# Attention step of a post-norm transformer layer: a new fixed order of the same instructions on all five queues

## The chip, the cores and the metric

The kernel runs on one core of a Trainium2 chip. The metric is the time of one execution on the device in microseconds (us), as the median of several runs. The engines of a core are TensorE (PE; its weight loads are listed apart as PEld), VectorE (DVE), ScalarE (ACT), GpSimd (POOL) and SyncE (SP, which only issues transfers). Each works through its own queue in order and waits on semaphores for the others.

## The reference, cut to what matters

```python
# x: (4, 1024, 256), 16 heads of 64
proj = x @ W_in.T + b_in                       # q, k, v
q, k = _rope(q, sin, cos), _rope(k, sin, cos)
att = einsum('bhqd,bhkd->bhqk', q, k) * scale  # causal mask, softmax
y = einsum('bhqk,bhkd->bhqd', att, v)
x = _layernorm(x + y @ W_out.T + b_out)
...
x = _layernorm(x + ffn(x))                     # 16 experts, top 3 of them by token
```

## The kernel before, in words

The program has four parts, one behind the other: attention, routing, experts, and the last sum with its norm. The change touches the first alone.

Attention is done for one pair of heads of one batch at a time: 4 batches by 8 pairs make 32 steps. A step is a set of named events, and its events are spread over several *turns* of a software pipeline. In each turn every engine runs through a fixed list of events, one list per queue. A mark behind an event tells of which step it is: none for the step of this turn, one + for the next step, ++ for the one after, - for the one before. So the lists alone decide in which order a queue works; what an event waits for is written in its own code and is the same wherever it stands. The turns are numbered from -2 to 32, and -2, -1, 0, 30, 31 and 32 are not full.

The events, by queue (q is 0 to 11, and .0 or .1 is the head of the pair):

- PE: **F** projections (F0, F1 for q and k, 12 matmuls of 512 columns; F2, F3 for v, 12 of 256). **A q.h** first-pass unit: scores for the maximum of each row (`a_ps`, L600). **X0, X1** transposes of the negated maxima (`t_ps`, L709). **B q.h** second-pass unit: the scores again, with the keys on the partitions, as two matmuls (`b_ps`, L607 and L608); its width goes 512, 384, 256, 128, 512 x5, 384, 256, 128 for q = 0 to 11. **V q** value product of both heads (`y_ps`, L689); V0 to V3 make one half of the output, V4 to V11 the other. **D** denominators (`t_ps`, L699). **O** output product, normalised values by W_out (`t_ps`, L714).
- ACT: **E q.h** the exponential of a second-pass unit (L799), **w** maxima out of `t_ps`, **h** the high half of roped q and k, **v**, **N**, **d** other evictions, **y** the norm of finished rows.
- DVE: **M q.h** maximum of a first-pass unit (L918, L922), **C** joins maxima, **r** the two products of the rotary embedding, **k** partial sums of probabilities (L956 to L961), **R** reciprocals, **G** multiplication by them (L971), **o** adds an output product to the rows (L981), **z** statistics of the norm.
- POOL: **a** and **l**, sum and low half of the embedding, **T** the causal cut of a diagonal block (L521), **K** partial sums (L535), **u** roots for the norm, **p** a bias.
- SP: **W** and **S** put the halves to memory and load them stacked, **L** loads weights and x.

The events V and D are matmuls with 64 output columns (`128*64` in the profile): the two heads lie side by side in TensorE's array. All others use 128 columns or, in X, 8. `a_ps`, `b_ps` have one bank per head, so that a unit waits until the unit before it of the same head has been read: A by M, B by E. `t_ps` is one bank for X, D and O, and each of these waits for the reader of the one before (`wait_misc`). The statistics z are there in the second and third turn behind the end of each of the first three batches, u in the fourth, y in the fifth and sixth, p in the third to the sixth.

Of the kernel before, what the change touches and what calls it, by code (L numbers as in the profile page):

```python
# [31 lines left out]
def parse(text):  # L32

    return [(w.rstrip("+-"), w.count("+") - w.count("-")) for w in text.split()]


PE_ORDER = parse("""B0.0 A0.0+ B0.1 A0.1+ A1.0+ B1.0 A1.1+ A2.0+ B1.1 X1 B2.0 A2.1+ A3.0+ B2.1 F0++ B3.0 A3.1+ D1- V8- V9- V10-
V11- B3.1 B4.0 A4+ B4.1 F1++ A5.0+ B5.0 V0 V1 V2 D0 V3 B5.1 B6.0 A5.1+ O1- A6.0+ B6.1 B7.0 X0+ A6.1+ B7.1
A7.0+ B8.0 V4 V5 V6 V7 B8.1 A7.1+ B9.0 O2- B9.1 B10.0 A8.0+ F2++ A8.1+ B10.1 A9.0+ O3- B11 A9.1+ A10.0+ O0
A10.1+ A11.0+ F3++ A11.1+""")  # L40
ACT_ORDER = parse("""E0.0 E0.1 E1.0 E1.1 E2.0 w1 E2.1 E3.0 d1- h0++ N1- E3.1 E4.0 E4.1 y0 h1++ E5.0 d0 h2++ E5.1 E6.0 N0 E6.1 y1 E7.0
w0+ E8.0 E7.1 h3++ E8.1 y2 E9.0 E9.1 y3 E10.0 v2++ E10.1 E11.0 E11.1 v3++""")
DVE_ORDER = parse("""M11.1 M0.0+ C0 M0.1+ M1.0+ M1.1+ M2.0+ k0 M2.1+ M3.0+ k1 k2 r0++ M3.1+ R4- r1++ R5- M4.1+ k3 M4.0+ R6- R7-
M5.0+ r2++ G1- r3++ z0 M5.1+ o1- M6.0+ R0 M6.1+ R1 M7.0+ R2 R3 G0 z1 M7.1+ o2- M8.0+ M8.1+ M9.0+ o3- M9.1+ M10.0+
o0 M10.1+ M11.0+""")
POOL_ORDER = parse("""K11- u0 T0 u1 T1 u2 T2 u3 a0++ l0++ T3 a1++ l1++ p0 a2++ l2++ K5 a3++ K6 l3++ K7 T8 T9 K8 T10 K9 T11 K10""")
SP_ORDER = parse("""L1+ S3+ L0++ W0++ S0++ W1++ S1++ S2++""")

UNITS = 12
ON_DIAGONAL = (0, 1, 2, 3, 8, 9, 10, 11)  # L50
# [3 lines left out]
LN_STATS, LN_ROOTS, LN_APPLY, LN_STORE = 1, 3, 4, 6  # L54
MISC = [(e, ahead) for e, ahead in PE_ORDER if e[0] in "XOD"]


def both(event):
    return [event + ".0", event + ".1"] if event[0] in "AB" else [event]


PE_ORDER = [(e, ahead) for event, ahead in PE_ORDER for e in ([event] if "." in event else both(event))]

# [30 lines left out]
def index_of(event):  # L94
    return int(event[1:].split(".")[0])
# [39 lines left out]
def attention_phase(nc, A, dram, shared):  # L135
# [4 lines left out]
    with ExitStack() as ctx:  # L140
# [120 lines left out]
        def turns(turn, order, last=None):  # L261
            for it in range(-2, STEPS + 1):
                turn(it, it % 4, last if last and it == STEPS else order)
# [8 lines left out]
        def _(sp):  # L272
# [117 lines left out]
            def turn(it, place):  # L390

                for i, (e, ahead) in enumerate(SP_ORDER):
                    n, s, c = it + ahead, (place + ahead) % 2, index_of(e)
# [54 lines left out]
        def _(pool):  # L448
# [87 lines left out]

            turns(turn, POOL_ORDER)

        @block.tensor
        def _(pe):  # L540
# [205 lines left out]

            turns(turn, PE_ORDER, PE_LAST)

        @block.scalar
        def _(act):  # L750
# [102 lines left out]

            turns(turn, ACT_ORDER, ACT_LAST)

        @block.vector
        def _(dve):
# [127 lines left out]
            dve.wait_ge(m["bias_in"], 16 * 9)  # L985
            turns(turn, DVE_ORDER)

# [861 lines left out]
```

## Time and profile before

| | |
|---|---|
| median of 3 runs | 1830.77 us (1829.52 to 1833.35) |
| the profiled execution | 1833.15 us, span 1831.4 us |
| busy in the span | PE 1685.0, DVE 1385.9, POOL 1232.3, ACT 729.2 us |
| attention, 60 to 1275 us | PE busy 1187.38 of 1215.00 us, DVE 1023.61, POOL 898.95, ACT 554.86; granted clock 0.99 |
| routing, 1275 to 1420 us | PE busy 104.12 of 145.00 us |
| experts and last sum, from 1420 us | PE busy 361.24 of 412.00 us |

In the timeline, a matmul's bar is longer than the time for which it holds the array, since matmuls overlap. What the next one has to wait is read from start to start. A row with "xN" holds N matmuls that follow each other.

### The profile page before, as it was taken

Reading aid. Unit: us, or ns where it says so; the run is one execution under the profiler, and the core shown is the slowest. Engines: PE = TensorE matmul, PEld = TensorE weight load, DVE = VectorE, ACT = ScalarE, POOL = GpSimd, SP = SyncE. Lnnn points to the kernel's source line nnn. Section 1 sums busy time; section 2 is a strip of 40 time slices with the busy share of each in tenths; the row PEclk is TensorE's granted clock in tenths of the full one; section 3 lists DMA queues with packets and bytes.
Section 4 is the critical chain, followed back from the end, with each engine's and each line's share of the span. In section 5 each row is a group of like instructions: output and inputs, shape, how many; then the busy total and the mean of one; then the engine's idle time right before and its main releaser. Section 6 shows DMA issues by size and latency. Waiting matters only on the chain. (4 is left out here: it accounts for less than half of the span.)

```text
span 1831.4 us, 34003 instructions
## 1 busy us (share of the span) xinstructions
PE 1685.0 (92%) x9489; PEld 1263.0 (69%) x9490; DVE 1385.9 (76%) x3230; ACT 729.2 (40%) x1549; POOL 1232.3 (67%) x1062
## 2 busy tenths in 40 slices
PE   4699999999999999999999999998659999999990
PEld 4566667666766677666766676664339999999980
DVE  3578888888888888988888888875775665665554
ACT  2234444444445544445444444543352222222222
POOL 3256788677877787788767787765016777777764
PEclk8799999999999999999999999999759999999995
DMA  9976566655665777556776565541964444444448
GB/s 303 343 204 164 156 167 200 182 168 154 186 161 165 232 220 199 147 170 192 204 236 187 161 186 149 153 113 49 337 191 69 74 71 73 74 72 71 73 63 277
DMA packets 185379, 302.10 MB, mean 165 GB/s; under 512 B 23600, under 2 KB 82736, under 8 KB 185120
## 3 DMA queue, kind: packets, MB, share of 16 engines
q1 hardware_dynamic: 161872, 269.20, 49.6%
q0 software_dynamic: 21312, 30.02, 10.3%
q10 hardware_dynamic: 2064, 1.31, 0.3%
q8 instruction: 60, 0.98, 0.2%
q14 instruction: 71, 0.58, 0.1%
HBM read 188.67 MB, written 111.54 MB: 164 GB/s over the span
## 5 line engine op out<-in xcount | busy, mean ns | idle before, releaser
L799 ACT ACTIVATE prob<-b_ps 128x512 f32<-128x512 f32 (+3 forms) x768 | 354.6, 488 | 354.7 <-PE b_ps L608 262.2
L535 POOL TENSOR_TENSOR acc<-acc,prob 128x1024 f32<-128x1024 f32 (+1 forms) x192 | 354.6, 1847 | 6.4 <-POOL acc L535 5.7
L607 PE MATMUL b_ps<-q,k 128*128 128x512 f32 (+3 forms) x768 | 294.9, 388 | 5.6 <-ACT prob L799 3.0
L508 POOL TENSOR_TENSOR roped<-rot 128x512 f32<-128x512 f32 x128 | 175.0, 1367 | 165.8 <-DVE rot L938 165.0
L600 PE MATMUL a_ps<-k,q 128*128 128x512 f32 (+3 forms) x768 | 266.0, 383 | 17.1 <-DMA k<-scratch_hilo 6.4
L918 DVE CUSTOM_DVE_ANT_0 masked<-a_ps,causal 128x256 bf16<-128x256 f32 (+3 forms) x512 | 245.9, 496 | 45.2 <-PE a_ps L600 37.8
L689 PE MATMUL y_ps<-prob,v_sb 128*64 128x512 f32 (+3 forms) x1536 | 274.2, 492 | 0.1
L608 PE MATMUL b_ps<-q,k 65*128 65x512 f32 (+3 forms) x768 | 264.7, 348 | 0.0
L1495 POOL DMA_INDIRECT scratch_sum<-y,dst_i x111 | 185.5, 1671 | 95.6 <-ACT y L1567 89.4
L967 DVE RECIPROCAL inv<-inv 128x128 f32<-128x128 f32 x256 | 232.2, 929 | 7.7 <-ACT inv L840 5.3
L513 POOL TENSOR_TENSOR lo<-roped,hi 128x512 fp32r<-128x512 f32 x128 | 176.1, 1376 | 80.3 <-ACT hi L812 80.3
L689 PEld LDWEIGHTS y_ps<-prob,v_sb 128*64 128x64 f32 x1536 | 104.6, 137 | 180.4 <-issue 175.6
L1521 PEld LDWEIGHTS h_ps<-mxT,w_now 128*128 128x128 f32 x1776 | 218.3, 194 | 5.6
L1521 PE MATMUL h_ps<-mxT,w_now 128*128 128x128 f32 x1776 | 218.7, 277 | 0.0
L1530 PE MATMUL yo_ps<-w,hT 128*128 x888 | 209.9, 379 | 0.0
L592 PE MATMUL g_ps<-xT,w_sb 128*128 128x512 f32 x768 | 194.1, 403 | 8.1 <-DVE rot L938 5.1
L607 PEld LDWEIGHTS b_ps<-q,k 128*128 128x128 f32 x768 | 145.2, 189 | 73.9 <-issue 42.8
L922 DVE TENSOR_REDUCE max_b<-a_ps 128x1 f32<-128x512 f32 (+1 forms) x256 | 163.1, 638 | 35.3 <-PE a_ps L600 32.8
L600 PEld LDWEIGHTS a_ps<-k,q 128*128 128x128 f32 x768 | 143.0, 192 | 59.7 <-DVE max_b L922 11.6
L1480 POOL DMA_INDIRECT xin<-scratch_xn,src_i x111 | 110.7, 997 | 106.0 <-POOLq L1009 72.5
L592 PEld LDWEIGHTS g_ps<-xT,w_sb 128*128 128x128 f32 x768 | 147.8, 196 | 40.3 <-DVE rot L938 6.2
L1530 PEld LDWEIGHTS yo_ps<-w,hT 128*128 128x128 f32 x888 | 160.1, 190 | 17.2
(258 smaller groups left out, 2396.3 us busy)
## 6 DMA issues: line engine op xcount, KB each, us to landing
q<-scratch_hilo SPq DMA_DIRECT2D x192, 256.0 KB, 4.5
k<-scratch_hilo SPq DMA_DIRECT2D x192, 256.0 KB, 5.2
scratch_hilo<-hi SPq DMA_DIRECT2D x64, 512.0 KB, 3.9
scratch_hilo<-lo SPq DMA_DIRECT2D x64, 512.0 KB, 4.6
w_sb<-scratch_wsplit SPq DMA_DIRECT2D x32, 512.0 KB, 3.6
w<-in_L_ffn_W_dram SPq DMA_DIRECT2D x32, 512.0 KB, 9.8
wv_sb<-scratch_wsplit SPq DMA_DIRECT2D x16, 512.0 KB, 6.0
xT<-scratch_xsplit SPq DMA_DIRECT2D x6, 1024.0 KB, 6.8
```

What stands on the lines that cost most here:

```text
L535: nc.gpsimd.tensor_tensor(sums, old, probs(q), ALU.add).then_inc(m["sum_p"], 1)
L592: ins = nc.tensor.matmul(out, left, right, start=(a, b, k) == PRODUCTS[0], stop=(a, b, k) == PRODUCTS[-1], skip_group_check=True)
L600: nc.tensor.matmul(out, q1[s][:, h, blk * P:(blk + 1) * P], k1[s][:, h, k0:k0 + w], start=True, stop=True, skip_group_check=True).then_inc ...
L607: nc.tensor.matmul(out, k1[s][:, h, js], q1[s][:, h, qs], start=True, stop=False, skip_group_check=True)
L608: ins = nc.tensor.matmul(out, k2[s][0:65, h, js], q2[s][0:65, half, h, 512 - w:512], start=False, stop=True, skip_group_check=True)
L689: ins = nc.tensor.matmul(y_ps[64 * h:64 * h + 64, 512 - w:512], v_sb[:, pairs, j, s, 64 * h:64 * h + 64], probs(q)[:, h, :], start=(j == 0 ...
L799: nc.scalar.activation(probs(q)[:, h, :], b_ps[:, h, 0:w], ACT.Exp).then_inc(exp_done[h], 1)
L918: nc.vector.tensor_tensor_reduce(masked[:, h, 0:w], a_ps[:, h, 0:w], causal[:, 512 - w:512], -1.0, -MASKED, ALU.add, ALU.min, out).then_in ...
L967: nc.vector.reciprocal(part, part).then_inc(inv_done[c], 1)
L1495: pool.indirect_dma_start(out=dram[f"sum{t % SUMS}"], out_offset=bass.IndirectOffsetOnAxis(ap=dst_i[:, t:t + 1], axis=0), in_=y[:, t % 2, ...
L1521: ins = nc.tensor.matmul(h_ps[:, s, c * P:(c + 1) * P], w1_now[:, s, k, c * P:(c + 1) * P], xT[:, s, k * P:(k + 1) * P], start=(k == 0), s ...
L1530: ins = nc.tensor.matmul(yo_ps[:, s, 0:D], hT[:, s, c * P:(c + 1) * P], w2[:, bass.ds(e, 1), c, :].rearrange("p a d -> p (a d)"), start=(c ...
```

## The change

The lists of the five queues are replaced. Nothing else is: the same events, the same waits, tiles and buffers.

```diff
-PE_ORDER = parse("""B0.0 A0.0+ B0.1 A0.1+ A1.0+ B1.0 A1.1+ A2.0+ B1.1 X1 B2.0 A2.1+ A3.0+ B2.1 F0++ B3.0 A3.1+ D1- V8- V9- V10-
+PE_ORDER = parse("""B0.0 A0.0+ B0.1 A0.1+ A1.0+ X1 B1.0 A1.1+ A2.0+ B1.1 A2.1+ B2.0 A3.0+ B2.1 F0++ B3.0 D1- A3.1+ V8- V9- V10- V11-
...
-DVE_ORDER = parse("""M11.1 M0.0+ C0 M0.1+ M1.0+ M1.1+ M2.0+ k0 M2.1+ M3.0+ k1 k2 r0++ M3.1+ R4- r1++ R5- M4.1+ k3 M4.0+ R6- R7-
+DVE_ORDER = parse("""M11.1 M0.0+ C0 M0.1+ M1.0+ M1.1+ M2.0+ k0 M2.1+ M3.0+ k1 r0++ M3.1+ R4- r1++ R5- M4.0+ M4.1+ R6- k2 R7- k3 r2++
...
-POOL_ORDER = parse("""K11- u0 T0 u1 T1 u2 T2 u3 a0++ l0++ T3 a1++ l1++ p0 a2++ l2++ K5 a3++ K6 l3++ K7 T8 T9 K8 T10 K9 T11 K10""")
-SP_ORDER = parse("""L1+ S3+ L0++ W0++ S0++ W1++ S1++ S2++""")
+POOL_ORDER = parse("""K11- u0 T0 u1 T1 u2 a0++ u3 l0++ T2 T3 a1++ p0 l1++ a2++ l2++ K5 a3++ K6 l3++ K7 T8 K8 T9 T10 K9 T11 K10""")
+SP_ORDER = parse("""L1+ L0++ S3+ W0++ S0++ S1++ W1++ S2++""")
```

PE in the first third of a full turn, before: B3.0, A3.1+, D1-, V8- to V11- (each V and D two matmuls, one for each head).

```order
L607 MATMUL b_ps<-q_0,k_0 128x128
L608 MATMUL b_ps<-q_0,k_0 128x128
L600 MATMUL a_ps<-k_1,q_1 128x512
L699 MATMUL t_ps<-acc,ones 64x512 x2
L689 MATMUL y_ps<-prob,v_sb 64x512 x2
L689 MATMUL y_ps<-prob,v_sb 64x384 x2
```

The same place of the changed kernel:

```order
L607 MATMUL b_ps<-q_0,k_0 128x128
L608 MATMUL b_ps<-q_0,k_0 128x128
L699 MATMUL t_ps<-acc,ones 64x512 x2
L600 MATMUL a_ps<-k_1,q_1 128x512
L689 MATMUL y_ps<-prob,v_sb 64x512 x2
L689 MATMUL y_ps<-prob,v_sb 64x384 x2
```

The first-pass unit A3.1+ has moved in between the denominators D1- and the value products. They stood as one stretch of 64-column matmuls, and are two now.

PE in the middle of the turn, before: B7.0, X0+, A6.1+, B7.1, A7.0+, B8.0, V4 to V7.

```order
L608 MATMUL b_ps<-q_1,k_1 128x512
L709 MATMUL t_ps<-ident,max_a 8x128
L600 MATMUL a_ps<-k_0,q_0 128x512
L607 MATMUL b_ps<-q_1,k_1 128x512
L608 MATMUL b_ps<-q_1,k_1 128x512
L600 MATMUL a_ps<-k_0,q_0 128x256
L607 MATMUL b_ps<-q_1,k_1 128x512
L608 MATMUL b_ps<-q_1,k_1 128x512
L689 MATMUL y_ps<-prob,v_sb 64x512 x8
L607 MATMUL b_ps<-q_1,k_1 128x512
```

The same place of the changed kernel: B7.0, A6.1+, V4, X0+, B8.0, A7.0+, B7.1, V5 to V7.

```order
L608 MATMUL b_ps<-q_1,k_1 128x512
L600 MATMUL a_ps<-k_0,q_0 128x512
L689 MATMUL y_ps<-prob,v_sb 64x512 x2
L709 MATMUL t_ps<-ident,max_a 8x128
L607 MATMUL b_ps<-q_1,k_1 128x512
L608 MATMUL b_ps<-q_1,k_1 128x512
L600 MATMUL a_ps<-k_0,q_0 128x256
L607 MATMUL b_ps<-q_1,k_1 128x512
L608 MATMUL b_ps<-q_1,k_1 128x512
L689 MATMUL y_ps<-prob,v_sb 64x512 x6
L607 MATMUL b_ps<-q_1,k_1 128x512
```

V4 stands alone, ahead of the transpose X0+, and B8.0 comes ahead of B7.1.

DVE in the first third of the turn, before: k1, k2, the two products of r0++, and M3.1+.

```order
L958 TENSOR_TENSOR acc<-prob 128x2x384
L961 TENSOR_TENSOR acc<-acc,prob 128x2x256
L938 SCALAR_TENSOR_TENSOR rot<-g_ps,bias,cos_sb 128x512
L938 SCALAR_TENSOR_TENSOR rot<-g_ps,bias,sin_sb 128x512
L918 ISA masked,max_a<-a_ps,causal 128x512
```

DVE of the changed kernel, some rows later: R5-, M4.0+ and M4.1+, R6-, k2, R7-, k3.

```order
L967 RECIPROCAL inv<-inv 128x128
L922 TENSOR_REDUCE max_b<-a_ps 128x1 x2
L967 RECIPROCAL inv<-inv 128x128
L961 TENSOR_TENSOR acc<-acc,prob 128x2x256
L967 RECIPROCAL inv<-inv 128x128
L961 TENSOR_TENSOR acc<-acc,prob 128x2x128
```

The partial sum k2 (`128x2x256`) has moved from ahead of r0++ to a place behind R6-, and k3, which stood behind M4.1+, follows it behind R7-. On POOL, T2, for which k2 waits, has moved behind l0++ in the same way (lists above).

## Rows read from the trace of the kernel before

**Rows 1.** Windows of one undisturbed and one long turn: busy us (x instructions), clock.

```profile
282.60:319.20 36.60, 36.60 (x195) 25.55 (x194) 31.84 (x67) 17.14 (x37) 28.66 (x25) 1.00 0.66 188
503.00:541.00 38.00, 36.98 (x196) 25.51 (x195) 31.69 (x69) 16.79 (x37) 32.74 (x41) 1.00 0.53 150
```

**Rows 2.** One line's instructions: X1, 95 to 1240 us (duration, first and last start).

```profile
L709 PE MATMUL t_ps<-ident,max_c x31: 272/273/275, 102.5 to 1211.2; 128*8 128x128 f32 x31
```

**Rows 3.** Timeline of PE in the undisturbed turn: start us, us, instruction.

```profile
299.88 1.03 PE L699 MATMUL t_ps<-acc,ones 128*64 128x512 f32 x4
300.74 0.39 PE L689 MATMUL y_ps<-prob,v_sb 128*64 128x128 f32 x4
...
304.02 0.39 PE L608 MATMUL b_ps<-q,k 65*128 65x512 f32 x1
304.25 0.27 PE L709 MATMUL t_ps<-ident,max_a 128*8 128x128 f32 x1
...
305.21 0.28 PE L600 MATMUL a_ps<-k,q 128*128 128x256 f32 x1
305.33 0.40 PE L607 MATMUL b_ps<-q,k 128*128 128x512 f32 x1
305.57 0.39 PE L608 MATMUL b_ps<-q,k 65*128 65x512 f32 x1
305.89 3.65 PE L689 MATMUL y_ps<-prob,v_sb 128*64 128x512 f32 x16
...
309.82 0.39 PE L608 MATMUL b_ps<-q,k 65*128 65x512 f32 x1
```

**Rows 4.** Timeline of all engines, same turn: the weight load of B7.1.

```profile
304.64 0.19 PEld L607 LDWEIGHTS b_ps<-q,k 128*128 128x128 f32 x1 [0.19 <-ACT prob L799]
```

**Rows 5.** Timeline, a turn with statistics z: B7.0 and X0+.

```profile
487.42 0.39 PE L608 MATMUL b_ps<-q,k 65*128 65x512 f32 x1
...
488.31 0.27 PE L709 MATMUL t_ps<-ident,max_a 128*8 128x128 f32 x1 [0.49 <-DVE x1b L981]
```

**Rows 6.** Timeline, the turn with roots u: B4.1.

```profile
515.67 0.47 PE L607 MATMUL b_ps<-q,k 128*128 128x512 f32 x1 [1.02 <-ACT prob L799]
```

**Rows 7.** Timeline, a turn with the norm y: A7.0+ and B8.0.

```profile
563.73 0.28 PE L600 MATMUL a_ps<-k,q 128*128 128x256 f32 x1
...
564.13 0.19 PEld L607 LDWEIGHTS b_ps<-q,k 128*128 128x128 f32 x1 [0.44 <-ACT prob L799]
```

**Rows 8.** Waits of 95 to 1208 us: us in total, times, longest us.

```profile
PEld b_ps L607 <- ACT prob L799: 8.9, 36, 0.5
...
PEld a_ps L600 <- DVE max_a L918: 8.1, 41, 0.4
PEld t_ps L709 <- DVE x1b L981: 8.1, 16, 0.9
...
PE b_ps L607 <- ACT prob L799: 2.1, 4, 1.0
```

**Rows 9.** Timeline, the first microseconds of the turn: M1.0+ ends, A2.0+ loads.

```profile
284.55 0.09 DVE L918 DVE_READ_ACCUMULATOR2_ANT max_a<- 128x1 f32 x1
284.69 0.19 PEld L600 LDWEIGHTS a_ps<-k,q 128*128 128x128 f32 x1 [0.16 <-DVE max_a L918]
```

**Rows 10.** Timelines of DVE (G1-, G0) and POOL (K6) in the undisturbed turn.

```profile
299.81 0.67 DVE L971 TENSOR_TENSOR yT<-yT,inv 128x512 f32<-128x512 f32 x1
308.92 1.25 DVE L971 TENSOR_TENSOR yT<-yT,inv 128x512 f32<-128x512 f32 x1
...
307.26 2.36 POOL L535 TENSOR_TENSOR acc<-acc,prob 128x1024 f32<-128x1024 f32 x1
309.59 1.72 POOL L513 TENSOR_TENSOR lo<-roped,hi 128x512 fp32r<-128x512 f32 x1
```

**Rows 11.** Timeline of POOL in turn 31: T9, then K8.

```profile
1265.88 0.41 POOL L521 TENSOR_SCALAR_AFFINE_SELECT prob<-prob 128x256 f32<-128x256 f32 x1 [1.05 <-ACT prob L799]
1266.25 2.35 POOL L535 TENSOR_TENSOR acc<-acc,prob 128x1024 f32<-128x1024 f32 x1
```

More of the change, by code:

```diff
@@ L34, in parse @@
     return [(w.rstrip("+-"), w.count("+") - w.count("-")) for w in text.split()]
-PE_ORDER = parse("""B0.0 A0.0+ B0.1 A0.1+ A1.0+ B1.0 A1.1+ A2.0+ B1.1 X1 B2.0 A2.1+ A3.0+ B2.1 F0++ B3.0 A3.1+ D1- V8- V9- V10-
[L38 to L42, printed above, removed]
-DVE_ORDER = parse("""M11.1 M0.0+ C0 M0.1+ M1.0+ M1.1+ M2.0+ k0 M2.1+ M3.0+ k1 k2 r0++ M3.1+ R4- r1++ R5- M4.1+ k3 M4.0+ R6- R7-
-M5.0+ r2++ G1- r3++ z0 M5.1+ o1- M6.0+ R0 M6.1+ R1 M7.0+ R2 R3 G0 z1 M7.1+ o2- M8.0+ M8.1+ M9.0+ o3- M9.1+ M10.0+
-o0 M10.1+ M11.0+""")
-POOL_ORDER = parse("""K11- u0 T0 u1 T1 u2 T2 u3 a0++ l0++ T3 a1++ l1++ p0 a2++ l2++ K5 a3++ K6 l3++ K7 T8 T9 K8 T10 K9 T11 K10""")
-SP_ORDER = parse("""L1+ S3+ L0++ W0++ S0++ W1++ S1++ S2++""")
+PE_ORDER = parse("""B0.0 A0.0+ B0.1 A0.1+ A1.0+ X1 B1.0 A1.1+ A2.0+ B1.1 A2.1+ B2.0 A3.0+ B2.1 F0++ B3.0 D1- A3.1+ V8- V9- V10- V11-
+A4+ B3.1 B4.0 F1++ A5.0+ B4.1 B5.0 A5.1+ V0 V1 D0 V2 V3 B5.1 B6.0 O1- A6.0+ B6.1 B7.0 A6.1+ V4 X0+ B8.0 A7.0+
+B7.1 V5 V6 V7 B8.1 A7.1+ O2- A8.0+ B9.0 A8.1+ B9.1 F2++ B10.0 B10.1 A9.0+ O3- B11 A9.1+ A10.0+ O0 A10.1+ A11.0+
+F3++ A11.1+""")
+ACT_ORDER = parse("""E0.0 E0.1 E1.0 E1.1 E2.0 w1 E2.1 E3.0 d1- h0++ N1- E3.1 E4.0 h1++ y0 E5.0 E4.1 d0 h2++ E5.1 E6.0 N0 E7.0 E6.1
+w0+ y1 E7.1 E8.0 h3++ y2 E8.1 E9.0 E9.1 y3 E10.0 E10.1 E11.0 E11.1 v2++ v3++""")
+DVE_ORDER = parse("""M11.1 M0.0+ C0 M0.1+ M1.0+ M1.1+ M2.0+ k0 M2.1+ M3.0+ k1 r0++ M3.1+ R4- r1++ R5- M4.0+ M4.1+ R6- k2 R7- k3 r2++
+G1- M5.0+ z0 r3++ M5.1+ o1- z1 M6.0+ R0 M6.1+ M7.0+ R1 R2 R3 G0 M7.1+ o2- M8.0+ M8.1+ M9.0+ o3- M9.1+ M10.0+ o0
+M10.1+ M11.0+""")
+POOL_ORDER = parse("""K11- u0 T0 u1 T1 u2 a0++ u3 l0++ T2 T3 a1++ p0 l1++ a2++ l2++ K5 a3++ K6 l3++ K7 T8 K8 T9 T10 K9 T11 K10""")
+SP_ORDER = parse("""L1+ L0++ S3+ W0++ S0++ S1++ W1++ S2++""")
 UNITS = 12
```

## The prediction

> **What bounds the kernel now.** I read the engines' busy shares first, then windows of one turn each, then TensorE's timeline in them, and last the list of waits. An undisturbed turn takes 36.60 us; TensorE is busy through all of it at the full clock of 2.4 GHz, DVE for 31.84, POOL for 28.66, ACT for 17.14 [rows 1]. So a turn ends when TensorE has worked through its list, and another engine counts where TensorE waits for it. Turns are not all that long: from the first X1 to the last, 30 turns later, 1108.7 us pass, 36.96 a turn [rows 2], and the longest fills its window of 38.00 without TensorE being busy throughout [rows 1]. The order can therefore act in two ways. It can change what a list costs TensorE when nothing is late, which repeats in every turn, and it can take away or bring waits, of which the bars hide many, so that they must be read from start to start.
>
> **The change, part one: boundaries.** Value products and denominators use 64 columns of the array, everything around them 128. Between the second halves of B8.0 and B8.1 lie 4.25 us (305.57 to 309.82) [rows 3]. Two second-pass matmuls at 0.24 each (305.33 to 305.57) and eight pairs of 64-column matmuls at 0.43 (299.88 to 300.74 is two pairs) come to 3.92. The stretch costs 0.33 us more than its work, for going in and coming out once. Before, a full turn has three such stretches: D1- with V8- to V11-, V0 to V3 with D0, V4 to V7. Now it has five, because A3.1+ stands between D1- and V8-, and X0+, B8.0, A7.0+ and B7.1 between V4 and V5. Moving D0 by one place inside its stretch, and O1-, O2- beside first-pass units, opens none.
>
> The first new boundary is there in the 30 turns that have both D1- and A3.1+. A3.1+ also loses a predecessor of 128 columns, which covers a weight load thinly, so I take 0.30 of the 0.33: 9.0 us. The second is there in 32 turns. There the array is left for a transpose with 8 columns of weights, where a load of 128 takes 0.19 [rows 4]; between 0.14 (all of that saved) and 0.33 I take 0.27, nearer the full price, since only the way out changes: 8.6 us. Together +17.6, and nothing hides it, for TensorE is the engine that never rests.
>
> The Trainium skill (TensorEngine Tiling (Array Packing), Key Properties) says that a change of tiling mode drains the engine, and gives no price. TensorE: Matmul & The Clock Gate puts the drain at some 128 cycles and a weight load at P / 1.2 ns; an estimate from it is 0.05 + 0.05 us going in and 0.05 + 0.11 coming out, 0.27 with rounding, so 62 boundaries would cost 16.7 at most. The sum above goes by the row.
>
> **Part two: waits that go.** B7.1 waits in undisturbed turns for its exponential E6.1, which stands on ACT behind the eviction N0 [rows 4]. In turns with the norm y, B8.0 waits for E7.0, which stands behind y1: 0.40 from A7.0+ to B8.0 against 0.12 [rows 7, 3], and the load in the open adds 0.1. Now V4, X0+, B8.0 and A7.0+ stand ahead of B7.1, and V4 (0.86 us) ahead of B8.0, and E7.0 ahead of E6.1 and y1. The waits of this pair come to 8.9 us in 36 [rows 8]. About three quarters of such a wait is lost time (0.38 of 0.44 in rows 7, less in the short ones), and some stand at the turn's start and stay: I take -6.
>
> X0+ must wait for o1-, which stands on DVE behind z0 in turns with statistics: 0.89 from B7.0 to it, against 0.23 [rows 5, 3], so 0.66 lost of a longest wait of 0.9. Its 16 waits are 8.1 us [rows 8]; 0.26 off each leaves 3.9. Behind V4 it comes 1.1 us later. All of it goes: -4. (On DVE, o1- itself comes later by z1 only behind it.)
>
> B4.1 waits for E3.1 in the turn with roots, since u0 to u3 hold up T2, k2, r0++, a0++ and h0++ one after the other: 1.02 us once, 2.1 in four waits [rows 6, 8], and some 0.1 each for the open load. Now r0++ stands ahead of k2, a0++ ahead of u3, and B4.1 stands behind F1. But l0++, T2 and so k3 come later, which D0 waits for, and a2++ and h2++, ahead of E5.1. Of 2.5 us I take back 1.5.
>
> At the end, turn 31 has no projections and waits on POOL's chain of sums. There K8 stands behind T9, which is 1.05 us late for its exponential [rows 11]; now K8 goes first: -1.0. Together -12.5.
>
> **Part three: waits that may come.** DVE used to do k2 while F0 ran; now its 0.7 us fall where DVE is full. Each of r2++, a2++ and h2++ comes a few tenths later, but so does TensorE, held up by the first boundary. E5.1 before B6.1, and k3 before D0, keep a few tenths of room. The tightest is A8.1+, which used to stand behind F2 and now stands ahead of it, 1.4 us earlier. It waits for M7.1+, which stands behind G0 on DVE. G0 takes 1.25 us and ends just after K6 on POOL does (309.62), while G1- takes 0.67 [rows 10]: a DVE sum of two SBUF operands stands still while POOL works. R1 to R3 now stand behind M7.0+, so G0 comes about 1 us later and may meet l3++ (1.3 us). Counting the queue through, A8.1+ would wait some 0.15 us in each of 29 full turns if it does, 0.3 at most, and nothing if it doesn't: 0 to 8.7, of which I take 2. X1 now stands two units earlier; it waits for C0, which ends in time in an undisturbed turn, and what it costs there is taken off the wait of A2.0+ behind it.
>
> The transfers move with the SP list (S3+ behind L0++, S1++ ahead of W1++), but are used a turn or more later: nothing, unless S3+ behind L0++'s wait for F1 came late, and it has half a turn.
>
> **The sum.** 17.6 - 12.5 + 2 = +7.1 us. On the profiled execution's 1833.15 that is 1840.3; it lies 2.4 above the median of the runs shown, so for the median I say 1830.8 + 7.1 = 1838.
>
> **The rivals.** *Slower still* (0.2): G0 meets l3++ in every turn and D0 or B6.1 wait too. For it: DVE is busy 31.84 of 36.60, and k2 lost its cover. Against: the longer turn gives the other engines 0.5 us more. 0.3 to 0.4 in 29 turns in place of the 2: 1845 to 1847.
>
> *No difference* (0.24): the boundary in front of or behind a single stretch costs less than that of the row, 0.2 say, since only two or four matmuls have to be covered, and all waits named go: 62 x 0.2 = 12.4, less 14 = -1.6, or some 1829 to 1834. The drain and loads that the Trainium skill's figures give lie between this and the row.
>
> *Faster* (0.11): the waits at the start of the turn go too. A2.0+ loads 0.05 us after M1.0+ ends at 284.64, having waited 0.16 [rows 9]; the waits for first maxima are 8.1 us in 41 [rows 8], and more lies hidden under the bars. X1, now in front, fills this time with work that had to be done anyway, and B2.0 follows sooner. If nothing else held F0 up, 0.3 us would come back in 29 turns: 1838 - 8.7 = 1829, and with the cheap boundary of the case before 1824. It decides at the start of F0: only if that comes more than 0.1 us sooner after B0.0 is it real. Against it: M1.0+, M1.1+ and M2.0+ follow each other on DVE without a gap, A3.0+ waits for M2.0+ as before, and their order has not changed.
>
> *As forecast* (0.45): 1834.5 to 1842.
>
> **Range and chances.** What a measurement of this kernel can tell from no change is about 0.2%, 3.7 us. Slower by more than that holds the forecast and the first rival, 0.65; within it 0.24; faster 0.11. Between 1829 and 1847 lies all but the faster rival and the far end of the slower one.
>
> **What would show it.** In the profile after: an undisturbed turn of 37.0 to 37.2 us; the second half of B3.0 to V8- longer by 0.3 besides the work that moved; V4 alone taking about 1.1 to 1.2 us until X0+; no wait of PEld of `t_ps` L709 for o1-, no 0.19 before B7.1; a wait of A8.1+ for `max_b` of 0 to 0.3; K8 in turn 31 right behind T8. I am wrong if a lone stretch costs under 0.2, if F0 starts sooner, or if a wait of over 0.3 us stands in every turn at a place that I have not named.

## The result: 0.7% slower, 1844.8 us against 1831.2

The changed kernel takes 1844.8 us in the median of 4 runs (1842.12 to 1845.83), the kernel before 1831.19 in the 4 runs beside them: a ratio of 1.0071, 95% interval 1.0054 to 1.0089, which is 10 to 16 us. The profiled execution of the changed kernel took 1843.8 us (span 1842.1), 10.7 above that of before. The forecast was +7, 1838, with a range to 1847.

On the page of the changed kernel PE is busy for 1691.9 us, DVE for 1380.7, ACT for 737.8 and POOL for 1229.4, much as before. Such sums tell nothing here; single turns do. Windows of an undisturbed turn, of a long one and of turns 1 to 29 together (columns as in [rows 1]; the third row has its match below it, from the kernel before):

```profile
400.48:437.48 37.00, 37.00 (x195) 25.52 (x194) 31.50 (x67) 17.40 (x37) 27.11 (x24) 1.00 0.59 172
288.24:325.94 37.70, 37.25 (x195) 25.33 (x194) 32.26 (x67) 17.25 (x37) 28.74 (x25) 1.00 0.62 182
138.56:1222.31 1083.75, 1077.25 (x5627) 737.29 (x5626) 930.46 (x1991) 514.16 (x1069) 826.54 (x736) 1.00 0.62 178
```

```profile
135.78:1208.48 1072.70, 1067.03 (x5627) 739.85 (x5626) 934.35 (x1991) 506.47 (x1069) 829.88 (x738) 1.00 0.63 180
```

Turns 1 to 29 are 11.05 us longer; the clock was full in both. Turn 1 also starts 2.8 us later (138.56 for 135.78), and behind turn 29 the changed kernel takes 3.1 us less, which together makes the 10.7 between the profiled executions. An undisturbed turn went from 36.60 [rows 1] to 37.00, inside the forecast 37.0 to 37.2, which makes 29 x 0.40 = 11.6. What turns take beyond that was 1072.70 - 29 x 36.60 = 11.3 us before, and is 1083.75 - 29 x 37.00 = 10.75 now. Here the forecast failed: it let most of the waits in disturbed turns go, and something as large has come instead.

**The boundaries.** PE's timeline in the undisturbed turn after, to be laid beside [rows 3]: D1- is alone between B3.0 and A3.1+, V4 between A6.1+ and X0+.

```profile
407.09 0.28 PE L608 MATMUL b_ps<-q,k 65*128 65x128 f32 x1
407.30 1.08 PE L699 MATMUL t_ps<-acc,ones 128*64 128x512 f32 x4
408.31 0.50 PE L600 MATMUL a_ps<-k,q 128*128 128x512 f32 x1
408.74 2.37 PE L689 MATMUL y_ps<-prob,v_sb 128*64 128x512 f32 x16
...
422.45 0.40 PE L600 MATMUL a_ps<-k,q 128*128 128x512 f32 x1
422.78 1.08 PE L689 MATMUL y_ps<-prob,v_sb 128*64 128x512 f32 x4
423.79 0.27 PE L709 MATMUL t_ps<-ident,max_a 128*8 128x128 f32 x1
```

The same place of the kernel before:

```profile
289.21 0.28 PE L608 MATMUL b_ps<-q,k 65*128 65x128 f32 x1
289.33 0.45 PE L600 MATMUL a_ps<-k,q 128*128 128x512 f32 x1
289.71 1.08 PE L699 MATMUL t_ps<-acc,ones 128*64 128x512 f32 x4
290.62 2.32 PE L689 MATMUL y_ps<-prob,v_sb 128*64 128x512 f32 x16
```

From the second half of B3.0 to V8- it was 290.62 - 289.21 = 1.41 us and is 408.74 - 407.09 = 1.65, 0.24 more, and the stretch that starts with V8- is 0.05 longer (2.37 for 2.32): 0.29 for D1-. V4 fills 1.01 us until X0+ (422.78 to 423.79), where its two pairs of matmuls take 0.86 inside a stretch [rows 3]: 0.15 more. A6.1+ to V4 takes 0.33, and a matmul of 512 columns 0.24 where no boundary follows: 0.09 on the way in. That makes 0.24 for V4 in this place, where the forecast took 0.27.

A start that comes sooner, which the "faster" rival wanted, is not there: F0 begins 3.80 us behind B0.0 (400.49 to 404.29), and it was 282.61 to 286.41 before. In the long turn it is 4.32 (288.25 to 292.57).

**The waits.** Waits in turns 1 to 29 of the kernel after (us in total, times, longest), beside [rows 8]. The waits of t_ps L709 for o1- (8.1 us in 16) are gone, as are PE's own 2.1 for the exponential. The 24 waits of PEld for an exponential are none of the old ones: they are B6.1's, 0.3 us, and B7.0's behind it, 0.19, in 12 turns. New are also that of X1 for `max_c`, in 12 turns, and A8.1+'s for `max_b`, in 2.

```profile
PEld b_ps L607 <- ACT prob L799: 6.0, 24, 0.3
PE t_ps L709 <- DVE max_c L929: 4.8, 12, 0.5
PEld a_ps L600 <- DVE max_b L918: 1.2, 2, 0.6
PE g_ps L592 <- DMA xT<-scratch_xsplit: 1.0, 2, 0.7
```

X1's wait stands in the long turns. The timeline of all engines in one of them shows K10 on POOL, the join C0 (L929) and M0.1+ behind it on DVE, then X1:

```profile
288.78 1.29 POOL L535 TENSOR_TENSOR acc<-acc,prob 128x512 f32<-128x512 f32 x1
...
289.27 0.82 DVE L929 TENSOR_TENSOR max_c<-max_b 128x8 f32<-128x8 f32 x1
...
290.02 0.28 DVE L918 CUSTOM_DVE_ANT_0 masked<-a_ps,causal 128x128 bf16<-128x128 f32 x1
...
290.25 0.27 PE L709 MATMUL t_ps<-ident,max_c 128*8 128x128 f32 x1 [0.45 <-DVE max_c L929]
```

C0 joins two lists of 8 values per partition, and takes 0.82 us: it ends at 290.09, with K10 (290.07). Its durations over the whole of attention (shortest, median, longest in ns, then first and last start):

```profile
L929 DVE TENSOR_TENSOR max_c<-max_b x31: 160/286/852, 99.7 to 1223.3; 128x8 f32<-128x8 f32 x31
```

### The profile page after: what moved, and what is told of

It reads as the page before. It is cut to its first block and busy times, and to the rows that moved or that the text cites. A ratio compares the mean times of both kernels' runs of the same rounds, so it can differ in the third digit from the quotient of the medians.

```text
span 1842.1 us, 34003 instructions
## 1 busy us (share of the span) xinstructions
PE 1691.9 (92%) x9489; PEld 1258.0 (68%) x9490; DVE 1380.7 (75%) x3230; ACT 737.8 (40%) x1549; POOL 1229.4 (67%) x1062
## 3 DMA queue, kind: packets, MB, share of 16 engines
q0 software_dynamic: 21312, 30.02, 10.2%
## 5 line engine op out<-in xcount | busy, mean ns | idle before, releaser
L535 POOL TENSOR_TENSOR acc<-acc,prob 128x1024 f32<-128x1024 f32 (+1 forms) x192 | 359.5, 1872 | 14.8 <-ACT prob L799 7.8
L600 PE MATMUL a_ps<-k,q 128*128 128x512 f32 (+3 forms) x768 | 276.5, 393 | 21.0 <-DMA k<-scratch_hilo 12.2
L607 PE MATMUL b_ps<-q,k 128*128 128x512 f32 (+3 forms) x768 | 284.0, 376 | 2.0 <-DMA q<-mrow 1.4
L689 PE MATMUL y_ps<-prob,v_sb 128*64 128x512 f32 (+3 forms) x1536 | 281.3, 494 | 0.0
L689 PEld LDWEIGHTS y_ps<-prob,v_sb 128*64 128x64 f32 x1536 | 99.0, 136 | 151.9 <-issue 125.8
L922 DVE TENSOR_REDUCE max_b<-a_ps 128x1 f32<-128x512 f32 (+1 forms) x256 | 157.1, 634 | 2.8 <-PE a_ps L600 2.8
```

What stands on the lines that cost most here:

```text
L535: nc.gpsimd.tensor_tensor(sums, old, probs(q), ALU.add).then_inc(m["sum_p"], 1)
L600: nc.tensor.matmul(out, q1[s][:, h, blk * P:(blk + 1) * P], k1[s][:, h, k0:k0 + w], start=True, stop=True, skip_group_check=True).then_inc ...
L607: nc.tensor.matmul(out, k1[s][:, h, js], q1[s][:, h, qs], start=True, stop=False, skip_group_check=True)
L689: ins = nc.tensor.matmul(y_ps[64 * h:64 * h + 64, 512 - w:512], v_sb[:, pairs, j, s, 64 * h:64 * h + 64], probs(q)[:, h, :], start=(j == 0 ...
```

## The experiments

All are timed beside the kernel before. Besides the ratio, the table has three times from the trace: from the first X1 to the last, 30 turns later (before: 1108.7 [rows 2]); turns 14 and 22, in which F1 needs the next batch's x; and the other 27 of turns 1 to 29, from each B0.0 to the next. The 27 turns repeat best: the changed kernel has 1007.2 and 1007.5 in its two traces, and 1007.9 and 1007.1 with another SP list. A difference there of more than a microsecond is taken for the edit's.

| kernel | median us | ratio (95%) | 30 turns | 27 turns | turns 14 and 22 |
|---|---|---|---|---|---|
| before | 1831.2 | 1 | 1108.7 | 999.0 | 73.7 |
| changed | 1844.8 | 1.0071 (1.0054 to 1.0089) | 1123.8 | 1007.2 | 76.6 |
| changed, once more | 1846.0 | 1.0073 (1.0057 to 1.0089) | 1123.5 | 1007.5 | 76.8 |
| changed, X1 back | 1846.4 | 1.0072 (1.0057 to 1.0086) | 1123.8 | 1005.5 | 78.9 |
| changed, C0 with one operand | 1842.0 | 1.0051 (1.0038 to 1.0064) | 1124.6 | 1002.3 | 82.4 |
| changed, old SP list | 1840.5 | 1.0046 (1.0032 to 1.0060) | 1120.3 | 1007.9 | 75.1 |
| changed, W1++ first on SP | 1838.8 | 1.0031 (1.0021 to 1.0042) | 1121.4 | 1007.1 | 75.1 |
| changed, both boundaries closed | 1842.3 | 1.0054 (1.0038 to 1.0070) | 1120.7 | 1005.5 | 75.8 |
| before, D1- apart | 1836.6 | 1.0023 (1.0013 to 1.0034) | 1113.0 | 1003.3 | 73.8 |
| before, V4 apart | 1841.6 | 1.0056 (1.0039 to 1.0072) | 1115.5 | 1005.8 | 74.2 |
| before, C0 with one operand | 1829.2 | 0.9984 (0.9973 to 0.9995) | 1107.0 | 997.8 | 73.2 |
| three mends | 1825.5 | 0.9965 (0.9951 to 0.9978) | 1105.3 | 992.7 | 75.9 |
| four mends | 1820.5 | 0.9930 (0.9915 to 0.9946) | 1102.3 | 992.0 | 73.2 |
| four mends, new SP list | 1825.0 | 0.9958 (0.9946 to 0.9970) | 1104.6 | 991.1 | 75.2 |

### Is it the place of X1?

```diff
-... A1.0+ X1 B1.0 A1.1+ A2.0+ B1.1 A2.1+ ...
+... A1.0+ B1.0 A1.1+ A2.0+ B1.1 X1 A2.1+ ...
```

> The changed kernel with X1 back behind B1.1 on TensorE, all else as changed. Theory 1 (the join C0 of the maxima, a DVE sum of two SBUF operands, stands still until POOL has ended K10, and everything behind C0 on DVE with it): X1 no longer waits, but A1.1+ and A2.0+ wait in its place for M0.1+ and M1.0+, which stand behind C0. Only 0 to 3 us of the 8.6 come back: 1842 to 1845 us. Theory 2 (the place of X1, ahead of units that could have run, is the cause): nearly all of it comes back, 1835 to 1837 us.

Nothing was gained in the median, which lies 1.4 us above theory 1's range and 9 above theory 2's; the 27 turns are 1.7 us shorter. The undisturbed turn stays at 37.00, the long one goes from 37.70 to 37.58. Its timeline shows the same C0, and who waits for it now:

```profile
288.41 1.29 POOL L535 TENSOR_TENSOR acc<-acc,prob 128x512 f32<-128x512 f32 x1
...
288.89 0.83 DVE L929 TENSOR_TENSOR max_c<-max_b 128x8 f32<-128x8 f32 x1
...
289.65 0.28 DVE L918 CUSTOM_DVE_ANT_0 masked<-a_ps,causal 128x128 bf16<-128x128 f32 x1
...
289.99 0.19 PEld L600 LDWEIGHTS a_ps<-k,q 128*128 128x128 f32 x1 [0.51 <-DVE max_a L918]
```

The first-pass unit A1.1+ stands still for M0.1+, which stands behind C0. So X1 is for the most part only the messenger: what costs is that the DVE queue is held.

### Is it POOL that holds C0?

The sum K10 reads two operands from SBUF, and so does C0. Here C0 reads one, seen as 8 pairs, with the same result:

```diff
-nc.vector.tensor_tensor(max_c[:, s], max_b[:, s, 0], max_b[:, s, 1], ALU.min)
+nc.vector.tensor_reduce(max_c[:, s].rearrange("p h i -> p (h i)"),
+                        max_b[:, s].rearrange("p q h i -> p (h i) q"), AX_X, ALU.min)
```

> The changed kernel, but C0 joins the two sets of maxima with a reduction that reads one SBUF operand, in place of a sum of two. The result is the same. Theory 1 (C0 is held by POOL's work because it reads two SBUF operands): C0 lasts 0.2 us or less in every turn, X1 waits no more, 8 to 9 us come back: about 1836 us. Theory 2 (C0 is late because DVE's queue is full): its start and the wait of X1 stay as they are, 1843 to 1846 us.

One line's instructions, then the timeline in the same turn, with K10, C0 and X1:

```profile
L929 DVE TENSOR_REDUCE max_c<-max_b x31: 165/166/168, 101.0 to 1225.7; 128x8 f32<-128x16 f32 x31
```

```profile
289.14 1.30 POOL L535 TENSOR_TENSOR acc<-acc,prob 128x512 f32<-128x512 f32 x1
...
289.60 0.17 DVE L929 TENSOR_REDUCE max_c<-max_b 128x8 f32<-128x16 f32 x1
...
289.96 0.27 PE L709 MATMUL t_ps<-ident,max_c 128*8 128x128 f32 x1
```

C0 is in the midst of K10 as before and takes 0.17 us; in no turn does it take more than 168 ns, where it took up to 852. X1 follows 0.36 us behind C0's start, not 0.98, and the turn takes 37.18, not 37.70. So the hold is shown, with its price: 0.5 us in a long turn, and 4.9 in the 27 turns (1002.3 for 1007.2). The Trainium skill (SBUF — State Buffer, Who interferes with whom) says that a DVE instruction with two SBUF inputs and a GpSimd instruction that reads SBUF exclude each other for a whole instruction, and that a `tensor_reduce` never contends on trn2. Both rows agree.

The median fell by 3.7 us of ratio (0.0020 x 1831), where theory 1 had expected 8 to 9, and the two intervals overlap; it is the 27 turns that tell. The trace also shows why a whole run tells so little: in turns 14 and 22 it took 5.8 us more than the changed kernel's, which have the same SP list, since F1 waited longer for a transfer:

```profile
PE g_ps L592 <- DMA xT<-scratch_xsplit: 4.8, 2, 2.6
```

The same edit in the kernel before, whose C0 also takes up to 696 ns:

> The kernel of before with C0 as a reduction of one operand. Theory 1 (POOL holds C0 also in some turns of before: A1.1+ waits 0.2 to 0.3 us more in about ten turns): 2 to 3 us less, 1828 to 1830 us. Theory 2 (C0 never counted before, since it ends in time): no difference, 1831 to 1832.

It gives 2.9 us (0.0016 x 1831), 1.7 in the 30 turns and 1.3 in the 27, as theory 1 said: A1.1+ waited for M0.1+ in 11 turns, by 0.2 to 0.4 us, and now does in none. Being held there is cheaper, since X1 stands further back and A1.1+ alone notices. So the change brought 4.9 - 1.3 = 3.6 us of it.

### What a boundary costs

First the kernel before with D1- alone ahead of A3.1+, then the kernel before with V4 alone ahead of B8.0.

```diff
-... B3.0 A3.1+ D1- V8- ...
+... B3.0 D1- A3.1+ V8- ...
```

> The kernel of before with one step of the change alone: D1- ahead of A3.1+ on TensorE. Theory 1 (a boundary costs 0.33 us by itself): 30 boundaries at 0.30 to 0.33, 9 to 10 us more, 1840 to 1842 us. Theory 2 (half of the loss per boundary is cover that other waits of the turn give back): 3 to 6 us more, 1835 to 1838.

```diff
-... A7.0+ B8.0 V4 V5 ...
+... A7.0+ V4 B8.0 V5 ...
```

> The kernel of before with V4 ahead of B8.0 and V5 behind it, nothing else moved. Theory 1: 32 boundaries at 0.33 (10.6 us), less the waits of B8.0 for E7.0 in the six turns with the norm (2.3 us), which V4 now covers: 8 us more, 1839 to 1841 us. Theory 2 (cheap boundary): 2 to 5 us more.

Windows of an undisturbed turn, of the first and of the second kernel:

```profile
281.88:318.76 36.88, 36.88 (x195) 25.54 (x194) 31.53 (x67) 17.03 (x37) 28.68 (x25) 1.00 0.64 187
```

```profile
320.74:357.68 36.94, 36.94 (x195) 25.44 (x194) 31.68 (x67) 17.00 (x37) 27.42 (x24) 1.00 0.67 199
```

Against 36.60 they cost 0.28 and 0.34 us a turn. D1- stands there as in the changed kernel, for 0.30 in the forecast. V4 does not: here a matmul of 128 columns follows it, in the changed kernel X0+, with 8. There its boundary costs 0.24, by the starts above and by undisturbed turns below. So the two come to 30 x 0.28 + 32 x 0.24 = 16.1 us in the changed kernel, for the 17.6 of the forecast.

In the whole kernel 4.2 and 10.3 us arrive (ratios), 4.3 and 6.8 in the 30 turns: theory 2 for D1-, and for V4 a little above theory 1. For D1- the waits show where the rest went: those of X0+ for o1- were 8.1 us in 16 [rows 8], and are

```profile
PEld t_ps L709 <- DVE x1b L981: 5.3, 10, 0.7
```

A longer list of TensorE gives the other queues 0.3 us more to be ready. The turns one by one bear it out: from B0.0 to B0.0, the eight of turns 1 to 29 that took 36.60 before are 0.29 longer each with D1- apart, and the other 21 only 0.10. The price of a boundary counts in full in undisturbed turns, and a turn which waits for another queue anyway can give part of it back.

### Closing both in the changed kernel

```diff
-... B3.0 D1- A3.1+ V8- ...
+... B3.0 A3.1+ D1- V8- ...
-... A6.1+ V4 X0+ B8.0 A7.0+ B7.1 V5 ...
+... A6.1+ X0+ B8.0 A7.0+ B7.1 V4 V5 ...
```

> The changed kernel with both new boundaries closed: A3.1+ ahead of D1-, and V4 behind B7.1 beside V5. Theory 1 (a boundary costs 0.33 us wherever it is, 62 of them 20 us): minus 20, plus up to 0.3 us a turn for the wait of B8.0 for E7.0, which V4 no longer covers: 1826 to 1834 us. Theory 2 (a lone stretch costs 0.2 or less): minus 12 at most, plus the same wait: 1833 to 1842 us.

It gained 3.1 us (ratio 1.0054 for 1.0071, with intervals that overlap), and 1.7 in the 27 turns, where the boundaries are worth some 16; at 1842.3 it lies above what either theory said. The undisturbed turn is 37.07 long, and PE is idle in it:

```profile
399.08:436.15 37.07, 36.73 (x195) 25.69 (x194) 31.13 (x67) 17.19 (x37) 27.13 (x24) 1.00 0.59 171
```

```profile
420.99 0.27 PE L709 MATMUL t_ps<-ident,max_a 128*8 128x128 f32 x1
421.60 0.50 PE L607 MATMUL b_ps<-q,k 128*128 128x512 f32 x1 [0.34 <-ACT prob L799]
```

B8.0 starts 0.61 us behind X0+ (0.03 in the changed kernel), waiting for the exponential E7.0. V4 had stood there as cover for it. So V4's boundary bought a cover that is worth more, 0.58 us for 0.24. By these rows, closing V4's boundary alone would lengthen the turn; no run did that.

### The SP list

```diff
-"""L1+ L0++ S3+ W0++ S0++ S1++ W1++ S2++"""
+"""L1+ S3+ L0++ W0++ S0++ W1++ S1++ S2++"""
```

> The changed kernel with the list of the transfer queue of before (S3+ ahead of L0++, W1++ ahead of S1++). Theory 1 (the 4.0 us for which A4.0+ waits for k in turn 0, and the waits of F1 in turns 14 and 22, come from the transfers' new order): they go, 3 to 5 us less, 1840 to 1842 us. Theory 2 (F1 simply comes earlier than before on TensorE, and turn 0 is late for another reason): 1844 to 1846 us.

> The changed kernel with one pair of the SP list back: W1++ ahead of S1++ as before, L0++ ahead of S3+ as after. It tells which of the two moves on SP costs the 4 us that the whole old list gave back. Theory 1 (W1++, which puts k's halves to memory, stood behind S1++, which waits for W0++'s data to land; so the halves of k come late in turn 0, where A4.0+ waited 4.0 us, and late in the turns that load the next batch's x): the wait of turn 0 goes and the median is 1840 to 1842. Theory 2 (L0++ ahead of S3+ is what costs: the load waits for F1 or for buffers and S3+ behind it): the 4 us wait stays and the median is 1843 to 1846.

The old list gives back 4.6 us of ratio (1.0046 for 1.0071), W1++ ahead of S1++ alone 7.3 (1.0031). Their intervals overlap, so this half of the edit seems to suffice. But of the two mechanisms that theory 1 named for it only one is there: F1's waits in turns 14 and 22 go, while A4.0+ still waits 3.5 us for k in turn 0. With the whole old list the median is where its theory 1 had it, and all waits for k in turn 0 are 3.1 us, for 5.3 in the changed kernel. In the 27 turns the list changes less than 1 us. Turn 1 starts at 136.5 to 140.0 us in the six traces with the new list, at 136.8 with W1++ first, and at 135.5 to 135.9 in the three with the old list and the other changed lists. SyncE's timeline shows why it can matter in turns 14 and 22. At the change of batch, S1 (first row; its issue has waited for W0's data), W1 (L337), S2 (L351) and the next x (L359) of the changed kernel, whose turn starts at 623.7:

```profile
614.10 0.57 SPq L348 DMA_DIRECT2D q<-scratch_hilo  x1
...
616.17 0.55 SPq L337 DMA_DIRECT2D scratch_hilo<-hi  x1
...
623.81 1.27 SPq L351 DMA_DIRECT2D q<-scratch_hilo  x2
...
629.14 0.61 SPq L359 DMA_DIRECT2D xT<-scratch_xsplit  x1
```

In the kernel before W1 (L337) is 4.9 us ahead of S2, in the changed one 7.6, and x leaves at 617.46, in a turn that starts at 615.6:

```profile
607.25 0.55 SPq L337 DMA_DIRECT2D scratch_hilo<-hi  x1
...
612.19 1.23 SPq L351 DMA_DIRECT2D q<-scratch_hilo  x2
...
617.46 0.56 SPq L359 DMA_DIRECT2D xT<-scratch_xsplit  x1
```

S2 waits for W1's data, the whole queue stands behind it, and x leaves 5.4 us into the turn instead of 1.8. The SP list accounts for two thirds of that: in the changed kernel x leaves at 3.1 with the old list and at 3.2 with W1++ first, the rest comes with the other queues' lists. F1 needs it some 12 us into the turn. The wait, in PE's timeline after:

```profile
636.37 1.85 PE L592 MATMUL g_ps<-xT,w_sb 128*128 128x512 f32 x7 [0.27 <-DMA xT<-scratch_xsplit]
```

Two more runs asked how steady that is: the changed kernel again, and the new SP list in the best kernel (below).

> The changed kernel itself once more, for a second trace and a second interval beside the run before. Theory 1 (the waits for transfers, F1's for xT and A4.0+'s for k in turn 0, differ from one execution to the next while everything else repeats): median 1842 to 1847, X1's and A2.1+'s waits as in the first trace to within 1 us, F1's wait somewhere between 1 and 9 us, A4.0+'s between 1 and 5. Theory 2 (the waits for transfers are set by the lists like all others): they come back as 1.0 and 4.0 us to within 0.3.

> The kernel with the four mends (median 1820.5 us with the old SP list), but with the SP list of the changed kernel: L0++ ahead of S3+, S1++ ahead of W1++. Theory 1 (S1++, whose issue waits for W0++'s data, stands ahead of W1++; so W1++, S2++ and the next batch's load of x come later, and F1 waits for xT twice in attention, each time by as much as the transfers take that day): 1824 to 1828, and F1 waits for xT in turns 14 and 22, 1 to 9 us in the two together. Theory 2 (the 3 to 7 us between the kernels with the one and the other SP list are how the chip ran, not the list): 1819 to 1822 and no such wait.

The repeat is 1.2 us longer in the median and 0.3 in the 27 turns, and its waits for transfers differ by up to 1.4 us from the first trace. That alone decides for neither theory; the 4.8 us of F1 in the trace of C0 with one operand, under the same SP list, speak for theory 1. F1's waits were 1.3 us in 2 and 1.5 us in 2, and none with the old list or W1++ first. The other difference is the wait for the first k: in the whole of attention PE waits for it

```profile
PE a_ps L600 <- DMA k<-scratch_hilo: 12.2, 4, 3.8
```

in the changed kernel, 10.8 in its second trace and 10.2 in the best kernel with the new list; 7.3 with the old list, 9.0 with W1++ first, 8.7 in the best kernel, 6.4 in the kernel before. But one trace of each is little to go by. F1's waits and those for k together are 9.1 us (both boundaries closed) to 16.7 (C0 with one operand) in the six traces with the new list, 12.3 in the mean, and 7.3, 8.7, 9.0 and 11.3 in the four of kernels with the changed lists and W1++ first, 9.1 in the mean. So the list is worth some 3 us by the waits, and in a single execution it can't be told. The best kernel lost 5.1 us by it (0.9958 for 0.9930), as theory 1 said, of which 1.5 are F1's and 1.5 those for k; the remaining 2 us are not accounted for. Nor does the list explain it all: the kernel with three mends has the old one, and its F1 waited 1.9 us, since x took 9.7 us to land in turn 14, for 7.1 in the changed kernel.

### The causes together, and a better kernel

The changed kernel with C0 on one operand, the old SP list, and A3.1+ ahead of D1- again:

> The changed kernel with three things mended: C0 as a reduction of one operand, the transfer list of before, A3.1+ ahead of D1-. If the causes add up (waits behind C0 some 6 to 8 us, transfers 4, one boundary in 30 turns 9): 1844.8 - 20 = 1824 to 1827 us, faster than both kernels. If they overlap or the freed time turns into waits elsewhere: 1830 to 1836.

1825.5 us, ratio 0.9965, 19 us under the changed kernel, where the 3.7 and 4.6 of the two single edits and D1-'s 30 x 0.28 = 8.4 make 17: the causes add up, as the first case said. In the 27 turns it is 14.4 us less. C0's edit gives 4.9 of them, and 9.5 are left for D1-, more than its 27 x 0.28 = 7.6. With it B6.1's waits go from all 12 turns (three others have one of 0.17), and a turn with that wait and without C0's hold took 37.17 to 37.19, some 0.17 above 37.00: 2.0 us. So what D1- ahead of A3.1+ cost in the changed kernel is its boundary and B6.1's wait. The undisturbed turn, 0.28 shorter than 37.00:

```profile
282.75:319.46 36.71, 36.71 (x195) 25.52 (x194) 31.15 (x67) 17.44 (x37) 28.98 (x25) 1.00 0.63 186
```

What is left of the change is a gain. Last, V4 as well goes back beside V5, now with its cover rebuilt: B7.1 in front of B8.0, and on ACT E6.1 in front of E7.0, as in the kernel before, but A6.1+ stays ahead of X0+.

```diff
-... A6.1+ V4 X0+ B8.0 A7.0+ B7.1 V5 ...     ACT: ... N0 E7.0 E6.1 w0+ y1 ...
+... A6.1+ X0+ B7.1 A7.0+ B8.0 V4 V5 ...     ACT: ... N0 E6.1 E7.0 w0+ y1 ...
```

> The kernel with the three mends (one-operand join of the maxima, the old SP list, A3.1+ ahead of D1- again), and now V4 too goes back beside V5: PE runs A6.1+ X0+ B7.1 A7.0+ B8.0 V4 V5, and ACT takes E6.1 ahead of E7.0 again, so that B7.1's exponential comes first. Theory 1 (a lone stretch of 64-column matmuls costs 0.33 to 0.35 us, and nothing covers for V4 here once the order of ACT and PE agree): 31 x 0.34 = 10 us less than the 1825.5 of the three mends, so 1815 to 1818, undisturbed turns of 36.4 us. Theory 2 (as in the kernel with both boundaries closed, the exponential that V4 covered comes late again, B7.1 or B8.0 waits 0.2 to 0.6 us in every turn, and X0+ waits in the turns with statistics): 1822 to 1830, undisturbed turns of 36.6 to 36.9 us.

1820.5 us, ratio 0.9930 (0.9915 to 0.9946): 13 us faster than before and some 26 faster than the changed kernel, between what the two theories said. Half of the gain over the kernel before lies in the 30 turns (1102.3 for 1108.7), the rest outside them. Turns 1 to 29, and the middle of an undisturbed turn:

```profile
135.45:1200.65 1065.20, 1063.16 (x5627) 743.94 (x5626) 908.71 (x1991) 514.10 (x1069) 829.27 (x738) 1.00 0.63 182
```

```profile
413.58 0.27 PE L709 MATMUL t_ps<-ident,max_a 128*8 128x128 f32 x1
413.72 0.50 PE L607 MATMUL b_ps<-q,k 128*128 128x512 f32 x1
...
414.96 3.65 PE L689 MATMUL y_ps<-prob,v_sb 128*64 128x512 f32 x16
```

B7.1 starts 0.14 us behind X0+, 0.11 late. The undisturbed turn is 36.58 long (391.68 to 428.26), as in the kernel before and 0.13 under that with three mends; with the 0.11 this is the 0.24 of V4's boundary. Yet the 27 turns are only 0.7 us shorter than with three mends (992.0 for 992.7), since A7.0+ now waits for a maximum in six of them. Most of the 5 us between the two medians is thus not V4's boundary; in the traces 2.7 lie in turns 14 and 22, where x leaves sooner.

What turns take beyond the undisturbed one is 1065.20 - 29 x 36.58 = 4.4 us, where it was 11.3 before. Some 7 us is what the change had to give in them, without its boundaries, together with C0's edit, which isn't part of it and gave the kernel before 1.7.

## Why the prediction was right in sign and range, and 6 us short

**Boundaries, 17.6.** Right in kind and near in size: 16.1, with 0.28 for D1- and 0.24 for V4 ahead of X0+. The reasoning for V4 is borne out: ahead of a matmul of 128 columns it cost 0.34, and ahead of the 8 columns of X0+ less. The estimate of 0.27 a boundary from the Trainium skill's figures lies between the two. The rival of the cheap boundary (0.2) fell with it. What failed is "nothing hides it, for TensorE is the engine that never rests": in the kernel before D1-'s boundary brought 4.3 us in place of 8.4, because disturbed turns gave part of it back. In the changed kernel, by the three mends, it counted in full.

**Waits that go, -12.5.** The waits for o1- went, as did B7.1's 0.19, those of B8.0 in turns with y, and PE's 2.1 for B4.1. That these went is read from the waits; what they were worth can be estimated from the 27 turns. They are 8.2 us longer than before. The boundaries make 27 x 0.52 = 14.0 of it, and what came new 3.6 (C0), 2.0 (B6.1) and 1.2 (A8.1+), so that some 12 to 13 must have gone, for 11.5 forecast there. In turn 31 K8 follows T8 at once, as forecast; what that brought no run tells apart.

**A8.1+, +2.** It waits in two turns, 18 and 26, by 0.6, not in 29. In the undisturbed turn there is no such wait, so the "slower still" rival fell too, although the time came to its 1845: for the most part by another mechanism. B6.1, which it named too, does wait, in 12 turns. At some 0.17 a turn that is 2.0 in all, where the forecast let E5.1 "keep a few tenths of room" and put nothing into the sum.

**X1, 0.** This is the step that failed in the turns: "it waits for C0, which ends in time in an undisturbed turn, and what it costs there is taken off the wait of A2.0+ behind it". The first half held, in undisturbed turns. But C0's durations, 161 to 696 ns, were to be seen in the kernel before, and I had named the mechanism for G0 and not asked it of C0, whose partner K10 stands in the turn's first microseconds. C0 held M0.1+ too, hence A1.1+ and A2.0+, so nothing was taken off. 12 waits of PE of up to 0.5 us stand for it. In the 27 turns it is 4.9 of the 8.2 us that they take beyond 37.00 each; B6.1's 2.0 and A8.1+'s 1.2 are the rest. 1.3 us of it was there before, so that 3.6 are new.

**Transfers, 0.** This is the step that failed outside them. "Used a turn or more later: nothing" looked at S3+ and L0++ and passed over that S2 waits for W1, and the next x stands behind both. It cost some 5 us by three comparisons of lists (4.6, 7.3, 5.1), of which the traces account for about 3.

**The sum.** 7.1 forecast, less 1.5 for the boundaries and 0.8 for A8.1+, with 3.6 from C0, 2.0 from B6.1 and 3 to 5 from the SP list, make 13 to 15; 13 were measured, with an interval of 10 to 16. The range, which went to 1847, held by 2 us: C0 and the transfers, both put at nothing, brought 7 to 9 us, more than half of the loss.

## What to carry to other kernels

Where a list has matmuls of two array shapes, keep each shape together: a stretch more cost 0.24 to 0.34 us a turn here. First look whether the piece in between is a cover, since closing both boundaries without another cover gave back 2 to 3 us of 16. Price such an edit in undisturbed and in held turns apart, and leave out turns that wait for transfers, which differed by up to 6 us between traces of the same lists. And when a short instruction's durations differ fivefold, ask who holds it before something is put behind it.

## What the runs showed that I had not expected

A join of 2 x 8 values per partition took 0.16 to 0.88 us in the changed kernel, by what POOL did at the time, and up to 1.29 in a variant of it; with a single operand it took 0.164 to 0.172 in every turn. It was not alone. DVE's groups by line in turns 1 to 29 (busy us, mean ns), of the changed kernel, of the one with C0 on one operand and of the one with four mends, where the edit of C0 moves the lines by one: the partial sums k2 and k3 (L961) and C0.

```profile
L961 DVE TENSOR_TENSOR acc<-acc,prob 128x512 f32<-128x512 f32 (+1 forms) x58 | 55.5, 958 | 0.0
...
L929 DVE TENSOR_TENSOR max_c<-max_b 128x8 f32<-128x8 f32 x29 | 13.3, 457 | 0.0
```

```profile
L962 DVE TENSOR_TENSOR acc<-acc,prob 128x512 f32<-128x512 f32 (+1 forms) x58 | 55.7, 960 | 0.0
```

```profile
L962 DVE TENSOR_TENSOR acc<-acc,prob 128x512 f32<-128x512 f32 (+1 forms) x58 | 44.1, 761 | 0.0
...
L929 DVE TENSOR_REDUCE max_c<-max_b 128x8 f32<-128x16 f32 x29 | 4.8, 166 | 0.0
```

C0 took 8.5 us less with its edit, and k2 and k3 11.4 less without any edit of theirs. C0 is not the cause of that: with its edit alone they take 55.7, as before it. In the kernel with both boundaries closed, where C0 still has two operands, they take 44.2, and in the one with three mends 44.1. Of the kernels with the changed DVE list, those with A3.1+ ahead of D1- on TensorE have the short ones, and the others the long ones. So the order of two events on TensorE took 11 us off DVE's busy time. That k2 then meets POOL less often is the likely reason, by C0's example, but no run took POOL's work away from it.
